# Three weight loads of a Mamba-and-BitLinear kernel move from GpSimd's DMA queue to the queues of SyncE and ScalarE

## What is computed

```python
xn = layernorm(x)
# the scan block (d_inner 2048, 16 states, chunks of 256 tokens that start from zero)
xc, res = split(xn @ W_in.T + b_in)             # 1024 -> 2 * 2048
u = silu(causal_conv3(xc) + conv_b)
dlt, B, C = split(u @ W_x.T)                     # 64, 16, 16
delta = softplus(dlt @ W_dt.T + b_dt)
state = exp(delta * A) * state + delta * B * u   # for each token of the chunk
y = sum over the 16 states of state * C
attn = (y * silu(res)) @ W_out.T + b_out
# the MLP: activations rounded to 8 bits, weights to -1, 0, 1 times a scale
ffn = bitlinear(silu(bitlinear(xn, w_gate)) * bitlinear(xn, w_up), w_down)
out = x + attn + ffn
```

## Time and profile before

| | |
|---|---|
| time, median of 3 runs | 5351.35 us (5346.89 to 5355.67) |
| the profiled execution's own time | 5355.32 us |
| its span (slowest core, core 2) | 5353.7 us |
| spans of the 8 cores | 5318.3 to 5353.7 us |
| granted TensorE clock, share of full | 0.656 to 0.661 |
| DVE, ACT, PE, POOL busy | 71%, 35%, 31%, 4% |
| DMA | 378 MB, 71 GB/s over the span |

### The profile page before, as it was taken

One profiled execution on the slowest core, in us unless ns is written; L12 is line 12 of the kernel. 1 busy time (PEld: TensorE's weight loads), 2 busy tenths in 40 slices (PEclk: granted clock), 3 DMA queues, 4 the chain that ended last, 5 costly groups with the idle time before them and its releaser, 6 DMA issues.

```text
span 5353.7 us, 46598 instructions; the slowest of 8 cores (5318.3 to 5353.7 us)
## 1 busy us (share of the span) xinstructions
PE 1676.2 (31%) x7308; PEld 847.1 (16%) x7308; DVE 3807.3 (71%) x10735; ACT 1860.2 (35%) x4106; POOL 209.8 (4%) x296
## 2 busy tenths in 40 slices
PE   0134210510231042114113211501200277786776
PEld 0022100200120021002001100300000023333332
DVE  3424888788778888887888888788888666664332
ACT  1335434334433434343332432333222122224332
POOL 0210000100000000000000000000000000000000
PEclk9996555755565565556556555755555589998998
DMA  6532103300320231033002100300100233330666
GB/s 227 163 85 60 36 0 102 98 9 20 109 80 0 75 99 36 0 114 103 0 0 71 44 0 8 99 1 0 48 0 0 77 117 97 118 96 20 204 212 196
DMA packets 229132, 378.37 MB, mean 71 GB/s; under 512 B 15522, under 2 KB 154914, under 8 KB 226724
## 3 DMA queue, kind: packets, MB, share of 16 engines
q1 hardware_dynamic: 194276, 236.98, 14.5%
q0 software_dynamic: 32832, 125.85, 7.4%
q10 hardware_dynamic: 1728, 12.58, 0.7%
HBM read 329.22 MB, written 46.14 MB: 70 GB/s over the span
## 4 chain that ended last, share of the span: by engine, by line
DVE 35%; DMA 18%; issue 18%; PE 17%; ACT 10%; DVEq 1%; SPq 0%; ACTq 0%; POOL 0%; POOLq 0%
DVE hbuf L677 11%; DVE dbub L670 5%; DVE ypb L699 4%; DMA wch<-s_winT 4%; ACT dAb L661 4%; DMA wdqt<-s_wdq 3%; DVE ypb L695 3%; PE psI L510 3%; PE psBC L640 2%; PE psP L1119 2%; DMA wo_buf<-s_woutT 2%; DVE yA L702 2%; DMA s_wdq<-wdstg 2%; PE psBC L647 2%; DMA wcf<-w_inT 1%
## 5 line engine op out<-in xcount | busy, mean ns | idle before, releaser
L677 DVE TENSOR_TENSOR_SCAN hbuf<-dAb,dbub 128x256 bf16<-128x256 bf16 x2048 | 1402.0, 685 | 275.2 <-ACT dAb L661 274.7
L661 ACT ACTIVATE dAb<-delta_t,alneg 128x256 bf16<-128x256 bf16 x2048 | 903.3, 500 | 24.6 <-DVE hbuf L677 24.3
L640 PE MATMUL psBC<-shstB,ones 1*128 1x256 f32 x256 | 142.2, 653 | 1920.8 <-DVE shstB L637 1920.8
L651 ACT ACTIVATE Bsb<-psBC 128x256 bf16<-128x256 f32 x128 | 49.2, 384 | 1871.1 <-PE psBC L647 1840.0
L670 DVE TENSOR_TENSOR dbub<-du_t,Bsb 128x256 bf16<-128x256 bf16 x2048 | 582.8, 285 | 6.0 <-ACT Bsb L651 2.4
L702 DVE TENSOR_TENSOR yA<-yA,ypb 128x256 f32<-128x256 f32 x1024 | 435.3, 425 | 109.5 <-DVE ypb L699 4.5
L510 PE MATMUL psI<-xnsc,wch 128*128 128x256 bf16 x2048 | 360.3, 352 | 244.0 <-DMA wch<-s_winT 220.9
L640 PEld LDWEIGHTS psBC<-shstB,ones 1*128 1x128 f32 x256 | 59.8, 289 | 1976.7 <-issue 1976.7
L699 DVE TENSOR_TENSOR ypb<-ypb,pa 128x256 bf16<-128x256 bf16 x896 | 261.8, 292 | 95.6 <-DVE ypb L695 3.2
L510 PEld LDWEIGHTS psI<-xnsc,wch 128*128 128x128 bf16 x2048 | 246.7, 125 | 355.0 <-issue 277.8
L752 PE MATMUL psOut<-wo_buf,gated 128*128 128x512 bf16 x256 | 123.4, 482 | 506.9 <-DVE gated L724 432.5
(11 more groups left out here) (157 smaller groups left out, 3520.4 us busy)
## 6 DMA issues: line engine op xcount, KB each, us to landing
wdqt<-s_wdq SPq DMA_DIRECT2D x64, 1024.0 KB, 6.8
wch<-s_winT SPq DMA_DIRECT2D x64, 512.0 KB, 5.3
wch<-s_winT POOLq DMA_DIRECT2D x64, 512.0 KB, 4.9
wo_buf<-s_woutT POOLq DMA_DIRECT2D x64, 512.0 KB, 4.8
wab<-wgT SPq DMA_DIRECT2D x32, 512.0 KB, 3.9
wab<-wuT SPq DMA_DIRECT2D x32, 512.0 KB, 4.2
wab<-wdT SPq DMA_DIRECT2D x32, 512.0 KB, 4.2
wqf<-wgT SPq DMA_DIRECT2D x64, 256.0 KB, 3.4
```

The lines of the kernel that those rows point to most:

```text
L640: P.op("tensor", lambda t, bk=bk: t.matmul(psBC[bk][:, 0:CH], ones2[64:65, 0:128], shstB[64:65, :], start=True, stop=True), reads=["shB", ...
L661: P.op("scalar", lambda s, q=q, n=n, b=b: s.activation(dAb[b][:], delta_t[p][:, q * CH:(q + 1) * CH], AF.Exp, bias=0.0, scale=alneg[:, q * ...
L677: P.op("vector", lambda v, b=b, b3=b3: v.tensor_tensor_scan(hbuf[b3][:], dAb[b][:], dbub[b3][:], 0.0, ALU.mult, ALU.add), reads=["dA:%d" % ...
```

## The change

Three loads get other issuing engines. Of the f32 weight tiles `wcf`, even ones go from ACT to SP and odd ones from POOL to ACT. Of the in-projection's groups `wch`, odd ones go from POOL to ACT. The out-projection's groups `wo_buf` go from POOL to SP. Nothing else is changed: not the program order, the sizes, the buffers or what waits for what. The stores stay on POOL.

```diff
--- before.py
+++ after.py
@@ -268,7 +268,7 @@
             for r in range(ntile):
                 for c in range(ncol):
                     b = wcnt % 2
-                    lq = "scalar" if wcnt % 2 == 0 else "gpsimd"
+                    lq = "sync" if wcnt % 2 == 0 else "scalar"
                     wcnt += 1
                     yield lambda src=src, r=r, c=c, b=b, cw=cw, lq=lq: P.op(
                         lq, lambda e: e.dma_start(
@@ -495,7 +495,7 @@
             writes=["xnsc:%d" % p], dma=True)
         for mg in range(16):
             wb = mg % 2
-            yield lambda mg=mg, wb=wb: P.op("sync" if mg % 2 == 0 else "gpsimd",
+            yield lambda mg=mg, wb=wb: P.op("sync" if mg % 2 == 0 else "scalar",
                 lambda e: e.dma_start(
                     wch[wb][:].rearrange("part (k c) -> part k c", k=8),
                     s_winT.ap()[:, mg * 256:(mg + 1) * 256].rearrange(
@@ -736,7 +736,7 @@
         for f in range(2):
             for kg in range(4):
                 wb2 = (f * 4 + kg) % 2
-                yield lambda kg=kg, f=f, wb2=wb2: P.op("gpsimd", lambda e: e.dma_start(
+                yield lambda kg=kg, f=f, wb2=wb2: P.op("sync", lambda e: e.dma_start(
                     wo_buf[wb2][:].rearrange("part (k c) -> part k c", k=4),
                     s_woutT.ap()[kg * 512:(kg + 1) * 512,
                                  f * 512:(f + 1) * 512].rearrange(
```

## The result

The changed kernel takes 5449.43 us (median of 8 runs, 5440.66 to 5462.29) against 5350.72 us before (8 runs on the same chip, 5342.1 to 5355.67): ratio 1.0188, 95% interval 1.0175 to 1.0201, 99 us slower. Forecast was slower, at 5390 (+39) with a range up to 5446. The sign is right; the size is two and a half times the forecast and 3 us outside its range. The nearest case was rival D.

The account below looks back on a forecast made before the run. DVE, busy 71%, was taken to matter most, with much of the end set by engines waiting in turn. The terms 38 + 15 + 22 - 8 - 28 = +39 us gave 5390 us, range 5337 to 5446.

Parts of the forecast that it names:

- rival D: As forecast, with 1 us more per wch load (+47), 3 us a chunk for delayed xnsc (+17): 5454 us; chance 0.09.
- two effects: Odd wch loads on ACT: sharing engines with SP's even load, and using a hardware queue; counted nothing, 1 us either way.
- First in-projection alone: In-projection ahead of all scans: late odd wch loads, covered by nothing, cost 22 us (15 to 29).
- First scan stage: In-projection inside the first scan (475 to 582 us): late odd wch loads cost 15 us (11 to 19).
- Six stages: Six similar in-projections woven into scans: late odd wch loads cost 6.4 us a stage, 38 us (17 to 74).
- wo_buf: -8 forecast: Out-projection loads answered sooner by SP: gain 10 to 20 us, less delays behind them; net -8 us (-20 to +3).
- the charge against it: In SP's queue, xnsc and the first wch load stand behind eight wo loads: 0 to 3 us a chunk.
- Cast stage: Weight casts at the start: wcf loads leave earlier, so DVE waits less; -28 us (-45 to -12).
- A: Cast stage speeds up to the layer norm's own pace, -98 us in place of -28: 5320 us; chance 0.07.
- B: Late wch loads are hidden in scans by ACT's lead; 38 and 15 fall to 0: 5337 us; chance 0.06.
- C: Issuing engine makes no difference, only the issue instruction's length counts: 7 us gained, 5344 us, no change; chance 0.10.
- The rule that stands beside it: Trainium skill's statement on DMA issue anywhere in the kernel: another issuing engine only saves the sequencer's time.

Follow-up runs that it names:

- The run without the overlap: Changed kernel with SP's even wch load waiting until ACT's odd one has landed: 5390.95 us, 1.0054 of the kernel before.
- the one with a single queue: Changed kernel with all wch loads on SP, odd ones held until the second eviction of the group before: 5379.17 us, 1.0033 of the kernel before.

## Why the prediction was wrong

**The failed step.** It is the sentence on two effects under "Odd wch loads, POOL to ACT": "I take nothing for the two, since the rows point both ways, and keep 1 us each way for the range." The lateness came about as worked out: POOL's load left 0.6 us after the matmuls that free its buffer, ACT's leaves 3.1 us after them (means on core 2), 2.5 us later where 2.8 was forecast. But it also lands in 6.1 us where POOL's landed in 4.9: 1.2 us for each odd load, above the 1 us kept. The price was to be had from a row it used elsewhere: at 243 GB/s a second 512 KB needs 2.2 us of the engines, so of two loads that leave together each may cost the other up to that; the prediction counted this for the xnsc load and for wcf, and not for wch. And the rows didn't point both ways. The 5.3 us of SP and the 4.9 of POOL in the earlier trace rows are medians of loads that travel beside each other, SP's mostly as the second. Where no other load is under way, POOL's lands in 4.6 us (17 loads of the kernel before, over the eight cores) and ACT's in 3.9 (56 loads of the changed one), the way in which the w_outT rows had pointed. So the move to ACT took 0.7 us off a load, and SP's load beside it put 2.0 on. The run without the overlap puts the overlap at 70 us or more, the one with a single queue at 81. The rest of wch's 162 us is then the late leaving: the single-queue run, in which the loads leave late, is 81 us above the one with wch back on POOL (5379.17 and 5298.52, same chip), where the prediction had 75. These are not exactly the same late loads: they leave 3.7 us after their buffer is free and land in 4.2, where ACT's leave 3.1 us after it and the prediction kept POOL's 4.9. The prediction gave rival D, which had 1 us more on each load, 9 in 100.

**A second missing amount, argued only.** PE's L510 took 25.5 us more on the profiled cores, 42 in the mean over the eight. The mean matmul took 312 ns with waits of 133 us, 352 with 221, 370 with 432 and 412 with 571, over four kernels; the kernel without the overlap stands a little out of that order, with 370 ns at 360 us. The granted clock of the first in-projection was 0.80 before (347.8 to 420 us) and 0.76 after. The prediction counted a clock only in the first in-projection. That the gaps lower the clock I read from the order of these rows; no run changed the clock by itself, and none shows how much of the 25.5 us reaches the end.

**Its terms.** By the starts of the gating step L724 at the end of each scan, on core 2:

- First in-projection alone: 22 forecast. It took 101.5 us on the profiled core for 72, so 29; in the mean over the cores 101.0 for 70.5. That is just past the 15 to 29. (Its 1.8 us for an even group at the full clock are 1.6 by its own two times, 374.92 and 376.5.)
- First scan stage: 15 forecast. With wch alone, chunk 0's gating starts at 1010.4 for 948.8, 61.6 later. The first in-projection starts 5.0 later there and takes 102.1 us for 72.1, which leaves 27 for the scan (28 in the mean over the cores); above the 11 to 19.
- Six stages: 38 forecast, 17 to 74. With wch alone the six periods last 2929.3 us for 2849.6, so +80 on core 2 (+114 on core 6, +106 in the mean over the eight). This is the term that was off most. The overlap above is in it; that the clock is too is argued.
- wo_buf: -8 forecast, -28 measured, outside -20 to +3. The gain that was forecast, 10 to 20 us of PE's wait, came as 8 in the mean over the cores, and DVE's wait for the results fell by 21.5. Wrong was the charge against it: with this edit alone, on core 2, PE's first in-projection matmul behind it starts at 983.9 us, where it had started at 984.4, though xnsc leaves SP only at 977. In the mean over the eight cores the six periods of the scans are 13 us shorter with this edit; where the rest of the 28 lies, the traces don't show.
- Cast stage: -28 forecast, -47 alone, just past -45 to -12. In the full change the in-projection starts 29 us earlier on the profiled cores and 35 in the mean over the eight; alone, on core 2, chunk 0's gating starts 36 us earlier. The engines had room: 272 GB/s for 243. What of the 47 lies behind that start isn't placed.

The forecast terms sum to +39; the parts measured on one chip to +81, and +99 for all.

**The rivals.** A fell: the stage gained 29 to 47 us, not 98. B fell: DVE's idle for dAb rose from 274.7 to 385.2 us over the kernel, so the scans didn't hide the loads. C fell by 256 us, the difference between wch's odd loads on ACT and on SP. The rule that stands beside it in the prediction (Trainium skill, DMA: Bandwidth & Descriptors, Issuing engines are not separate DMA queues) is half of the matter: the loads do share the engines, as the landings show, but the list of the issuing engine decides when a load leaves and the queue has a part in who is served first. D was right in its 1 us for each load, wrong in its 17 us for xnsc.

**The signs named ahead.** PE's waits for wch of 6 to 8 us: 6.3 to 8.4. The first in-projection 103 us: from its first matmul 101.5, where the forecast's 103 counted 8 us of the first wait as well, so it is longer by 29 and not 22. Casts ended before 220 us: 212. DVE's idle in a stage of 92 us up to 24 or more: 21.2 in 92 us on the profiled core, so not met as written; but the stage itself is longer, and over the whole of it (106 us for 91 on core 2) DVE idles 31.0 us for dAb, where it had been 18.4.

## What to carry to other kernels

When a load moves to another engine's list, find the instruction that stands ahead of it there, and compare when that one starts with when the buffer comes free: the difference is the prefetch that is lost. Then look for what else leaves at that moment: here two loads that left together from two queues both landed late, the later of them last, and in one queue the first was spared. So put the load that is needed first in front, in the same queue; by the landings the order did more of it here than the queue. A queue with nothing else in its list (SP here) is the place for loads that must run ahead; and try the parts of such a change singly, since two gains of 28 and 47 us were hidden in this one.

## What the runs showed of the hardware

The same 512 KB load of wch took these medians from issue to landing: 4.0 us from ACT with none beside it, 4.3 us with all on SP's queue, 4.9 from POOL and 5.3 from SP with the kernel before's stagger, 6.1 from ACT and 5.5 from SP when the two leave together. ACT's queue gave both the shortest and the longest, so what is beside a load decides more than its queue. POOL's queue is slower by itself: with no other load under way its load took 4.6 us (17 loads of the kernel before), two of SP's in the same kernel 3.9. The number of packets for the same bytes did change with the queue. Packets, MB and share of the 16 engines by queue (q0 is POOL's), before and then changed:

```profile
q1 hardware_dynamic: 194276, 236.98, 14.5%
q0 software_dynamic: 32832, 125.85, 7.4%
q10 hardware_dynamic: 1728, 12.58, 0.7%
```

```profile
q1 hardware_dynamic: 229796, 283.12, 17.0%
q10 hardware_dynamic: 68288, 46.14, 3.0%
q0 software_dynamic: 12672, 46.15, 2.4%
```

79.7 MB left POOL's queue with 20,160 packets and came to the hardware queues with 102,080. The engines' time for all of it stayed at 22.6 and 22.4% of the span, so five times the packets cost the engines next to nothing here.
